# Two additions for q stand in turn with the two scalings of k on GpSimd, in every second tile

## What is computed

```python
qkv = x @ Wqkv                      # after a shift of half the channels by one token
q, k, v = split(qkv)                # 16 heads of 64
q = l2norm(q) * qs;  k = l2norm(k) * ksc
q = q * cos * scale + rotate_half(q) * sin * scale
k = k * cos / scale + rotate_half(k) * sin / scale
sim = einsum(q, k2) * 8.0           # 32 queries of a window, 64 keys: its own and the window before
attn = softmax(where(mask, -max, sim))
x = x + (einsum(attn, v2)) @ Wo
x = x + ffn(layernorm(shift(x)))    # GELU-gated, 128 -> 2 x 341 -> 128
```

## Time and profile before

| | |
|---|---|
| timed runs, median (lowest to highest) | 3657.97 us (3655.81 to 3658.06) |
| profiled execution | 3635.34 us, span 3633.5 us |
| busy share of the span | PE 93%, PEld 74%, DVE 77%, ACT 70%, POOL 78% |
| mean granted clock of PE | 0.975 of full speed |
| tile loop | about 595 to 3550 us of the span |

### The profile page before, as it was taken

How to read it: one execution, slowest core, us unless ns; L and a number is a source line. 1 busy time by engine, 2 the same in 40 slices (tenths; PEclk the granted TensorE clock), 3 DMA queues, 4 the chain that set the end, 5 groups by cost and what they waited for, 6 DMA issues and landing times.

```text
span 3633.5 us, 148686 instructions
## 1 busy us (share of the span) xinstructions
PE 3380.5 (93%) x64228; PEld 2686.8 (74%) x64228; DVE 2807.8 (77%) x4876; ACT 2530.0 (70%) x4686; POOL 2818.6 (78%) x3470
## 2 busy tenths in 40 slices
PE   3799986999999999999999999999999999999997
PEld 2566543788878888777888787887888877878775
DVE  3487666888888888888888888888888888888873
ACT  3333223778777888787887787887878877878763
POOL 1455546998888888888888888888888887888872
PEclk9899997999999999999999999999999999999998
DMA  3323211211111111111111121111111111111110
GB/s 101 105 92 94 86 33 54 55 42 41 46 48 49 42 43 43 47 44 47 44 39 46 49 52 39 43 43 50 46 47 41 42 44 49 39 43 47 36 43 24
DMA packets 126733, 183.46 MB, mean 50 GB/s; under 512 B 29824, under 2 KB 61440, under 8 KB 126080
## 3 DMA queue, kind: packets, MB, share of 16 engines
q1 hardware_dynamic: 119232, 146.15, 15.9%
q0 software_dynamic: 6848, 27.80, 2.4%
HBM read 59.01 MB, written 14.16 MB: 20 GB/s over the span
## 4 chain that ended last, share of the span: by engine, by line
PE 72%; POOL 8%; ACT 7%; issue 5%; DVE 4%; DMA 1%; SPq 0%; POOLq 0%; ACTq 0%; DVEq 0%
PE bank L548 17%; PE bank L611 9%; PE bank L622 8%; PE bank L584 7%; PE bank L558 5%; PE bank L595 4%; PE bank L685 3%; PE bank L663 3%; PE bank L674 3%; ACT big L1364 2%; ACT sq L1338 2%; PE bank L568 2%; POOL S L1686 1%; PE bank L523 1%; PE bank L463 1%
## 5 line engine op out<-in xcount | busy, mean ns | idle before, releaser
L548 PE MATMUL bank<-wqkv,xs 128*128 128x512 f32 x3456 | 1057.7, 422 | 19.3 <-DVE m L1017 13.6
L1678 POOL TENSOR_TENSOR m<-m 128x512 f32<-128x512 f32 x576 | 729.2, 1286 | 30.4 <-DVE m L1017 27.8
L548 PEld LDWEIGHTS bank<-wqkv,xs 128*128 128x128 f32 x3456 | 583.9, 191 | 103.7 <-issue 12.8
L1338 ACT ACTIVATE sq<-bank 128x512 f32<-128x512 f32 x768 | 458.9, 597 | 92.4 <-PE bank L548 54.5
L1017 DVE TENSOR_TENSOR m<-bank,tab 128x512 f32<-128x512 f32 x768 | 521.9, 680 | 0.3 <-POOL m L1678 0.3
L1686 POOL TENSOR_TENSOR S<-S,nw 128x1024 f32<-128x1024 f32 x192 | 383.4, 1997 | 172.9 <-DVE S L1048 172.9
L1028 DVE TENSOR_REDUCE ss<-sq 128x8 f32<-128x512 f32 x768 | 505.2, 675 | 0.0
L1694 POOL TENSOR_TENSOR S<-S,rs 128x512 f32<-128x512 f32 x384 | 411.6, 1093 | 52.9 <-DVE rs L1062 50.4
L611 PEld LDWEIGHTS bank<-P,big 64*64 64x64 f32 x24576 | 382.2, 136 | 79.9 <-issue 72.8
L1015 DVE TENSOR_TENSOR m<-bank,tab 128x512 f32<-128x512 f32 x576 | 392.5, 682 | 62.5 <-ACT sq L1338 47.1
L611 PE MATMUL bank<-P,big 64*64 64x32 f32 x24576 | 404.9, 221 | 3.5 <-issue 2.7
(11 more groups left out here) (229 smaller groups left out, 6628.5 us busy)
## 6 DMA issues: line engine op xcount, KB each, us to landing
big<-vst SPq DMA_DIRECT2D x1536, 64.0 KB, 2.0
stage<-in_wqkv SPq DMA_DIRECT2D x36, 256.0 KB, 2.9
tab<-in_tab SPq DMA_DIRECT2D x48, 128.0 KB, 2.2
xsort<-big SPq DMA_DIRECT2D x4, 960.0 KB, 8.9
big<-xsort SPq DMA_DIRECT2D x12, 256.0 KB, 6.3
ysort<-big SPq DMA_DIRECT2D x12, 256.0 KB, 3.6
wo<-in_wo SPq DMA_DIRECT2D x6, 512.0 KB, 3.5
big<-in_x SPq DMA_DIRECT2D x8, 256.0 KB, 3.4
```

The source lines that it names most:

```text
L548: m = eng.matmul(pb[:, :], xt[a], wqkv[:, z, 512 * part:512 * part + 512], start=(n == 0), stop=(n == 2))
L1338: eng.activation(sq[:, part % 2, :], bank[part % 2][:, :], ACT.Square, scale=1.0, bias=0.0).then_inc(s["a_sq"], 1)
L1678: eng.tensor_tensor(turned(g, part), turned(g, part), m2[:, part % 2, :], ALU.add).then_inc(s["g_add"], 1)
```

## The change

In iterations of even n, `add(n, 0)` stands ahead of `scale(n-2, 0)` and `add(n, 1)` between the two scalings. In iterations of odd n the order stays. No operation is added or removed.

```diff
                 weighed(n - 3)
+                if n % 2 == 0:
+                    add(n, 0)
                 scale(n - 2, 0)
+                if n % 2 == 0:
+                    add(n, 1)
                 scale(n - 2, 1)
-                add(n, 0)
-                add(n, 1)
+                if n % 2 == 1:
+                    add(n, 0)
+                    add(n, 1)
                 divide(n - 3, 0)
                 divide(n - 3, 1)
```

## The result

| | before | changed |
|---|---|---|
| timed, median (lowest to highest) | 3656.89 us (3643.23 to 3658.06) | 3693.28 us (3687.98 to 3697.26) |
| ratio, 95% interval | | 1.0103 (1.0087 to 1.0118) |
| profiled execution | 3635.34 us | 3697.26 us |
| mean granted clock of PE | 0.975 | 0.972 |

The change makes the kernel slower by 1.0%: 37.7 us on 3657, with an interval of 31.8 to 43.2. The forecast was 46.3 us, and 3704 in all. The two profiled executions lie 61.9 us apart, but that is too much to put down to the change. Here are all uses of the scaling of the even tiles' k (L1672) in the changed kernel: minimum, median and maximum in ns, then first and last start in us.

A forecast was written before the change was run, and what follows sets the result against it. PE was taken to bound the kernel, with no room in middle rounds. Delays of 32.0 + 4.9 us in tiles with n divisible by 4 and 9.4 in the first eight even tiles gave 3658.0 + 46.3 = 3704.3 us; range 3683 to 3718.

The forecast's parts named there:

- What bounds the kernel: Middle rounds of four tiles: PE busy 59.21 of 59.40 us, so any new delay to PE lengthens the round.
- First scaling covered with nothing left over: POOL, even tiles: first scaling ends 1.27 us later, about 2600.05, just before PE's first turning of k at 2600.08.
- Second turning 1.12 us late: PE, tile 132: second scaling ends 2.54 us later, so the second turning of k starts at 2602.34, not 2601.22.
- The 1.1 us is not won back in the tile: PE behind the second turning: `sim` also 1.1 us late, and back-to-back work recovers none of it.
- The first eight even tiles: n = 2 to 16, uneven tiles: delays of 0.14 to 1.76 us each, 9.4 us together.
- The sum: All tiles: 32.0 + 4.9 + 9.4 = 46.3 us of added delay, with bounds of 37 and 55.
- Tiles with n % 4 == 2: From n = 18 on, PE comes to k later, 1.2 us of margin remain, so no cost.
- the q additions' readers: DVE's second product and PE's turning of q: additions end 1.0 and 2.05 us earlier, but no gain.
- B: Rival: PE's pauses in `sim` swallow part of the delay, 16.7 us in 17 tiles, giving 3688; chance 0.12.
- C: Rival: earlier q additions return 9.8 us of PE's waits and k's delay hides, giving 3648; chance 0.04.
- D: Rival: POOL's ends are rough and the true margin exceeds 2.5 us, so no change, 3658; chance 0.06.
- E: Rival: each new PE standstill lowers the granted clock, 60 us on top in 37 tiles, 3764; chance 0.04.

The follow-up runs named there:

- E11: The changed kernel run once more with no edit, against the kernel before: ratio 1.0097 (1.0080 to 1.0115), 35.3 us.
- E12: The kernel before run once more with no edit, as if it were another: ratio 0.9996 (0.9982 to 1.0009).
- E1: Kernel before, even tiles reordered to scale 0, add 0, add 1, scale 1, so only the second scaling moves: ratio 1.0108 (1.0075 to 1.0142).
- E5: Kernel before with the changed order only in tiles with n % 4 == 0: ratio 1.0103 (1.0072 to 1.0133), 37 us.
- E2: Kernel before, even tiles reordered to add 0, scale 0, scale 1, add 1: ratio 1.0029 (1.0015 to 1.0043), 10.6 us.
- E3: Kernel before, even tiles reordered to add 0, add 1, scale 0, scale 1: ratio 1.0155 (1.0121 to 1.0190), 56 us.
- E9: Kernel before with the changed order only in 17 tiles with a PE pause behind the second turning of k: ratio 1.0030, 10.9 us.
- E4: Kernel before with the changed order only in tiles with n % 4 == 2: ratio 1.0010 (0.9995 to 1.0025), 3.6 us.
- E6: Kernel before with the same order of four in odd tiles only: ratio 0.9986 (0.9971 to 1.0001).
- E8: Changed kernel with the last six of the chain's twelve steps left out: ratio to the kernel before 0.9975 (0.9962 to 0.9988).
- E7: Kernel before, its order kept, with the last six of the chain's twelve steps left out: ratio 0.9962 (0.9946 to 0.9978).

## Why the prediction was right, point by point

- What bounds the kernel: right. PE had no room in the middle rounds, and a stop of PE lengthened them nearly one for one (1.12 us late, 0.98 us longer, or 0.8 to 1.0 with the traces of E11 and E12).
- First scaling covered with nothing left over: right (2600.11 against 2600.08), and E1 finds no share for it.
- Second turning 1.12 us late: right to the digit of the trace. E5 puts nearly the whole cost in the tiles with n divisible by 4, E1 at the second scaling, and E2 and E3 show the threshold from both sides: 1.27 us goes into the cover, and 2.54 us on the first turning costs 1.32 a round.
- "The 1.1 us is not won back in the tile": a little is. In the kernel before, `sim` starts at 2602.55 and the turning of q at 2604.09, 1.54 us. In the changed kernel it is 2652.75 and 2654.17, 1.42. The second traces have 1.52 (E12) and 1.41 (E11), and over the tiles without a pause it is 0.1 us each. That is 0.1 x 37, 3.7 us of the sum, and the pauses give back 2.3 more (4.0 less 1.7, under E9). Both terms I had at nothing.

Turning of q in the first tile and `sim` of the tile n = 18, before and then changed:

```profile
601.32 1.94 PE L558 MATMUL bank<-kc,m 128*128 128x128 f32 x8 [0.78 <-ACT vst L1346]
...
847.16 1.48 PE L584 MATMUL bank<-big,qT 64*32 64x64 f32 x128
```

```profile
616.09 1.94 PE L558 MATMUL bank<-kc,m 128*128 128x128 f32 x8 [0.78 <-ACT vst L1346]
...
868.70 1.48 PE L584 MATMUL bank<-big,qT 64*32 64x64 f32 x128
```

- The first eight even tiles: 252.61 less 245.84 is 6.8 us (6.5 by E11 and E12), where the sum had 9.4. There the waits fold into each other, as the lower bound allowed. A term mis-sized by 2.6.
- The sum: 46.3 - 3.7 - 2.3 - 2.6 = 37.7, inside the interval of the timed comparison (31.8 to 43.2) and of E11 (29.1 to 41.9). That it meets the measured 37.7 to the digit is luck, as the intervals are 11 us wide and more. The forecast of 3704 was 11 too high, 8.6 for these terms and the rest for the scatter of the runs, and the range held. PE's own waits for the scalings say about the same: 42.8 us in place of 7.0, 35.8 more.
- Tiles with n % 4 == 2 and the q additions' readers: no cost and no gain, right (E4; E6 for the odd ones).
- B, C, D and E: B in full falls with E9, and some 2 of its 16.7 us are there. D falls with the waits for L1672, and C too, since nothing became faster. What C rested on, PE's wait before the turning of q at 3216.55, looks like one of the pauses: an instruction packet landed at 3215.01, 1.54 us before, and the addition named as releaser had ended at 3212.85. E falls with the clock of 1.00 in the changed round, in which PE stops for 0.90 us, and with the timed runs: the mean granted clock of E11's is 0.9736 and that of the kernel before, in the same comparison, 0.9735. The Trainium skill (TensorE: Matmul & The Clock Gate, Part 1) lets the clock fall when PE has been idle; the trace has no fall after a stop of this length.
- The Trainium skill's rule of instruction blocks fetched ahead (Runtime: NRT & Kernel Launch, Instruction fetch mechanics) stood beside B in the prediction. The trace agrees that instructions come by DMA in blocks of 16 KB. Against what B needed, the blocks that end the pauses start behind the stop (E9), and `sim` still pauses for more than 0.7 us in 29 places of the changed kernel.

## What to carry to other kernels

A step that is moved behind others on a queue costs its lateness less the margin at its reader, and that margin differs from tile to tile when the work of an iteration does: read it in each kind of tile, where the engine in question arrives last. Two late steps that feed one engine in order can cost the worse delay and not the sum (E3). A margin can be made by making the queue's engine arrive earlier (E8), until the next wait, hidden before, sets its start.

Of the kernels run, the one with the half chain and the order of before (E7) is the fastest, 0.4% below the kernel before. It leaves out the second refinement of the roots, so whether it can be used hangs on the precision that is wanted.

## What the runs showed that I had not expected

- Two traces of the same kernel differ by 9 us in the tile loop (2913.1 and 2922.1 us from first to last scaling), and the changed kernel's two in the part ahead of the loop by 14 us (first scaling at 633.9 and 619.5). A difference of two single traces isn't a cost of a change, tile by tile excepted.
- When PE has stood still ahead of it, the next run of 128 short matmuls and what follows it start closer together: 1.42 us in place of 1.54 at n = 132, and 0.1 us less on average over 20 tiles.
